# Rotated heads stored the other way round, fewer and larger stack transfers, and a new order of work at the layer borders

## What is computed

```python
xn = layernorm(x)
x = x + attn0(xn, Wq, Wk, Wv, Wo) + ffn0(xn, w_gate, w_up, w_down)      # 16 heads of 32, causal, rotary; hidden 2048
xn = layernorm(x)
x = x + attn1(xn, ...) + ffn1(xn, gate_w, up_w, down_w, scales)         # 16 heads of 32, causal, rotary; hidden 1408
# ffn(xn) = (silu(xn @ gate.T) * (xn @ up.T)) @ down.T
```

## Time and profile before

| | |
|---|---|
| median of 3 runs | 2055.16 us |
| the profiled execution's own time, and its span | 2055.59 us, 2053.8 us |
| PE, DVE, ACT, POOL busy | 91%, 54%, 52%, 34% of the span |
| mean granted clock of TensorE | 0.958 of full speed |
| DMA | 126.2 MB, 22% of 16 engines' time |

### The profile page before, as it was taken

How to read it: one execution, slowest core, us unless ns; L and a number is a source line. 1 busy time by engine, 2 the same in 40 slices (tenths; PEclk the granted TensorE clock), 3 DMA queues, 4 the chain that set the end, 5 groups by cost and what they waited for, 6 DMA issues and landing times.

```text
span 2053.8 us, 25605 instructions
## 1 busy us (share of the span) xinstructions
PE 1866.4 (91%) x8656; PEld 1347.6 (66%) x8656; DVE 1116.6 (54%) x2432; ACT 1060.1 (52%) x2353; POOL 703.4 (34%) x516
## 2 busy tenths in 40 slices
PE   4999999999899899898889999999988998998987
PEld 3777767775675666656467777776757756575654
DVE  6554647373755564736346465573746636455452
ACT  2464646556256473646425646464652555646363
POOL 3225243242341533333213243534314415233320
PEclk9999999999999899999779999999999999999989
DMA  4213113031130313103213131311401403121201
GB/s 159 67 42 98 42 44 90 27 99 41 52 88 22 87 47 73 42 21 109 72 62 78 37 92 42 84 56 29 122 11 52 101 9 98 42 68 37 66 7 41
DMA packets 59874, 126.20 MB, mean 61 GB/s; under 512 B 9440, under 2 KB 10464, under 8 KB 58720
## 3 DMA queue, kind: packets, MB, share of 16 engines
q1 hardware_dynamic: 59744, 124.57, 22.0%
HBM read 69.48 MB, written 4.19 MB: 36 GB/s over the span
## 4 chain that ended last, share of the span: by engine, by line
PE 69%; DVE 11%; ACT 6%; SPq 5%; issue 5%; POOL 3%; DMA 2%; DVEq 0%; ACTq 0%; POOLq 0%
PE D L905 15%; PE G L905 11%; PE U L905 8%; PE OE L999 7%; PE SS L983 6%; PE OE L905 6%; PE SS L905 6%; SPq L564 5%; PE OE L983 3%; PE OE L962 3%; PE SS L962 2%; DVE OE L826 2%; ACT OE L618 2%; ACT pr L634 2%; DMA QS<-pr 1%
## 5 line engine op out<-in xcount | busy, mean ns | idle before, releaser
L874 DVE TENSOR_TENSOR xres<-D,xres 128x512 f32<-128x512 f32 x352 | 243.1, 691 | 214.1 <-PE D L905 209.7
L634 ACT ACTIVATE pr<-SS 128x512 f32<-128x512 f32 (+3 forms) x512 | 232.2, 501 | 143.8 <-PE SS L983 135.5
L709 POOL TENSOR_TENSOR hl<-tt,hh 128x512 fp32r<-128x512 f32 x108 | 139.0, 1287 | 475.7 <-ACT hh L651 475.7
L618 ACT ACTIVATE OE<-OE,mp 128x384 f32<-128x384 f32 (+3 forms) x256 | 203.4, 795 | 104.9 <-DVE mp L826 104.0
L826 DVE CUSTOM_DVE_ANT_0 OE<-OE,mask 128x384 f32<-128x384 f32 (+3 forms) x256 | 220.5, 873 | 50.6 <-PE OE L962 49.7
L618 ACT ACTIVATE SS<-SS,mp 128x128 f32<-128x128 f32 (+3 forms) x256 | 162.2, 634 | 95.7 <-DVE mp L826 94.0
L728 POOL TENSOR_SCALAR_AFFINE_SELECT pr<-pr 128x512 f32<-128x512 f32 x128 | 81.0, 635 | 378.7 <-ACT pr L634 378.7
L826 DVE CUSTOM_DVE_ANT_0 SS<-SS,mask 128x128 f32<-128x128 f32 (+3 forms) x256 | 167.6, 673 | 64.3 <-PE SS L962 63.0
L905 PE MATMUL G<-xh,wgh 128*128 128x512 f32 x432 | 178.0, 412 | 24.0 <-DVE tt L885 22.8
L983 PE MATMUL SS<-QS,KS 98*128 98x512 f32 (+2 forms) x512 | 182.1, 413 | 14.9 <-ACT pr L634 12.3
L905 PE MATMUL D<-wdh,hh 128*128 128x512 f32 x432 | 174.2, 403 | 19.6 <-DVE xres L874 13.7
(11 more groups left out here) (123 smaller groups left out, 3733.6 us busy)
## 6 DMA issues: line engine op xcount, KB each, us to landing
KS<-pr SPq DMA_DIRECT2D x192, 128.0 KB, 2.3
QS<-pr SPq DMA_DIRECT2D x192, 128.0 KB, 2.3
raw<-in_wgate_dram SPq DMA_DIRECT2D x27, 512.0 KB, 3.7
raw<-in_wup_dram SPq DMA_DIRECT2D x27, 512.0 KB, 3.7
raw<-in_wdown_dram SPq DMA_DIRECT2D x27, 512.0 KB, 3.7
raw<-in_wqk_dram SPq DMA_DIRECT2D x16, 512.0 KB, 4.4
val<-in_x_dram SPq DMA_DIRECT2D x4, 1024.0 KB, 6.9
trig<-in_wv_dram SPq DMA_DIRECT2D x4, 1024.0 KB, 5.6
```

The costliest lines, as they stand in the source:

```text
L618: act.activation(s, s, ACT.Exp, bias=mp[:, c, at:at + 1], scale=-1.0, accum_out=se[:, c, at:at + 1]) \
L634: act.activation(weights(i)[:, h, skip:W], SB[(i * HG + h) % 3][:, skip:W], ACT.Exp, scale=-1.0) \
L709: pool.tensor_tensor(hl[:, fc, :], tt[:, (blk * nfc + fc) % 2, :], hh[:, fc, :].bitcast(F32), ALU.subtract) \
L874: dve.tensor_tensor(xres[:, rt, :], d[:, :], xres[:, rt, :], ALU.add).then_inc(sem["v_dfree"], 1)
```

## The change

- **Order of heads.** The split of the Q and K weights writes its columns in the order (dimension, head) (`heads_apart`), so partition k*4+h of a projection holds dimension k of head h. The shuffle is i ^ 4, and the rotation tables are loaded by four transfers with a partition step of 4 instead of one.
- **Order of the projections.** t = 0 to 3 is now K first half, Q first half, K second half, Q second half. After each `rotate`, SyncE issues three transfers that carry all four heads (128 partitions into 32 by 4 heads by 512 columns): 12 a turn of 256 KB instead of 24 of 128. The first natural score waits for the first six (`d_stack`), the 17th for the others (`d_later`).
- **Borders.** The output products of the last turn's second half become items, in front of the norms. `v_weights` comes after the second norm instead of in front of the first scaled tile. The next layer's first projection and first value product (`early`) are taken out of the opening and put in front of the last down products. `keep` is a transfer from DRAM, issued by SyncE. The chain for 1/sqrt keeps its scratch in the PSUM bank `S[1]`. In the opening, `norm` 5, 6 and 7 stand together behind the second projection.
- **Start.** SyncE loads the first four row tiles one by one, the first Q/K weights and the value weights, and only then sets the semaphores and loads the constants. Only the Q/K weights are split in front of the walk; the other three blocks follow after the first norms (`first`).
- **The logarithm's guess** is two ScalarE instructions; VectorE has none in it.
- **Splits on GpSimd** are cut in instructions of 512 columns.
- **Pieces.** `GU_PARTS` stays 2. All 16 digit strings are new, and the late down pieces of the last group stand after three pieces instead of two. Waits are dropped where a stronger one stands in front (`st`, `gated`, `add`).

```diff
+        def heads_apart(kind, t):
+            return t.rearrange("p (g k h) -> p g h k", h=HG, k=DH) if kind == "A" else t
...
-    items.append([("pv", n - 2), ("pv", n - 1), ("heads", 1)])
+    items += [[("pv", n - 2), ("pv", n - 1), ("heads", 1)] + [("x_next",)] * (l == 1 and not final)] + output(1)
...
-    pieces += g0[:GU_PARTS] + late + g0[GU_PARTS:] + g1[:GU_PARTS]
+    pieces += g0[:3] + late + g0[3:] + g1[:3]
     if l == 0:
         rows = [piece + [("row", 1, rt)] for rt, piece in enumerate(d0)]
         rows[-1] += normal(1)
-        pieces += rows + g1[GU_PARTS:] + output(1) + [piece + [("row", 1, TPC + i)] for i, piece in enumerate(d1)]
+        pieces += rows + g1[3:] + early(1) + [piece + [("row", 1, TPC + i)] for i, piece in enumerate(d1)]
         items += norms(1, range(TPC))
+        items[-3].append(("v_weights", 1))
     else:
         d0[-1].append(("store", 0))
         d1[-1].append(("store", 1))
-        pieces += d0 + g1[GU_PARTS:3 * GU_PARTS]
+        pieces += d0 + g1[3:9]
         if not final:
-            items[-1] += [("x_next",), ("v_weights", 0)]
             items += [[("row", 0, rt) for rt in range(TPC)] + normal(0)] + norms(0, range(TPC))
+            items[-3].append(("v_weights", 0))
             pieces[-1].append(("keep", 0))
-        pieces += output(1) + g1[3 * GU_PARTS:] + d1
-    return opening(l), items, pieces
+        pieces += g1[9:] + (early(0) if not final else []) + d1
+    first = opening(l)
+    if (b, l) != (0, 0):
+        first = [x for x in first if [x] not in early(l)]
+    return first, items, pieces
+def early(layer):
+    return [[("proj", 0, True)], [("values", 0, layer)]]
...
-    return [("stats", layer, 0)] + [("v_weights", 1)] * layer + [("xn", layer, 0), ("xn", layer, 1)]
+    return [("stats", layer, 0), ("xn", layer, 0), ("xn", layer, 1)]
...
+    proj = [("proj", t, True) for t in range(2 * NC)]
+    values = [("values", rt, layer) for rt in range(RT)]
...
+    out = [("row", 0, rt) for rt in range(TPC, RT) if layer == 0]
+    out += [("stats", layer, 1), ("xn", layer, TPC), ("xn", layer, TPC + 1), proj[0], values[0], values[1], ("rotate", 0)]
+    out += values[2:4] + later[0] + [proj[1]] + later[1] + later[2] + later[3] + [("keep", 1)] * (layer == 0) + [values[4]]
+    return out + [*values[5:], ("rotate", 1), proj[2], ("rotate", 2), proj[3], ("rotate", 3)]
+START = [("row", 0, rt) for rt in range(TPC)] + normal(0)
+START += [("v_weights", 0)] + [x for piece in norms(0, range(TPC)) for x in piece] + [("first",), ("keep", 0)]
...
-        ("00500010101001100112021102021111111020010020010000100100000100100001000010010000010010001001000000000",
-         "00700010101001100112021102021111111020010020010000100100000100100001000010010000010010001001000000000",
+        ("01200011000100011003020302110202111010101001000000100101000100100000000010010000010010000011000000000",
+         "00400000100020002012020311111111102001010010010000140010001001000000000010010000010010000011000000000",
...
+            for rt in range(TPC):
+                sp.dma_start(val[:, rt, :], x[0, rt * P:(rt + 1) * P, :]).then_inc(d_tile[rt], 16)
+            load(sp, "A", 0, raw[:, 2, :], "raw2")
+            sp.dma_start(wv_raw, wv[0].rearrange("p (c n) -> p c n", c=KC)).then_inc(sem["d_wv"], 16)
...
-                if t % NC < NC - 1:
-                    return
-                qk = t // NC
+                qk, c = t % 2, t // 2
+                cols = slice(c * W, (c + 1) * W)
                 flats = ((flat_h, flat_h, flat_l), (flat_h, flat_l, flat_h))[qk]
                 sp.wait_ge(sem["g_rl"], n("g_rl", 1))
                 if qk:
                     sp.wait_ge(sem["p_v"], n("p_v"))
-                for h in range(HG):
-                    for r, src in enumerate(flats):
-                        at = slice(r * DH, (r + 1) * DH)
-                        sp.dma_start((QS[at, :, h, :] if qk else KS[at, h, :]).bitcast(F32),
-                                     src[qk][h * DH:(h + 1) * DH, :]).then_inc(sem[f"d_stack{h}"], 16)
+                for r, src in enumerate(flats):
+                    at = slice(r * DH, (r + 1) * DH)
+                    sp.dma_start((QS[at, c, :, :] if qk else KS[at, :, cols]).bitcast(F32), src[qk][:, cols]) \
+                        .then_inc(sem["d_later" if c else "d_stack"], 16)
...
+            def keep(n, c):
+                sp.wait_ge(sem["d_out"], n("d_out"))
+                sp.dma_start(xres[:, c * TPC:(c + 1) * TPC, :], rows(x, n, c, n.batches)).then_inc(sem[f"d_keep{c}"], 16)
...
-                act.wait_ge(sem["v_lse"], n("v_lse", 2))
+                act.wait_ge(sem["a_nat"], n("a_nat"))
+                act.activation(y0[:, :], se[:, c, :].bitcast(I32), ACT.Copy, scale=LN2 / 2 ** 23, bias=-(127 - 0.043) * LN2).then_inc(sem["a_log"], 1)
+                act.wait_ge(sem["a_log"], n("a_log", 1))
                 act.activation(ex[:, :], y0[:, :], ACT.Exp, scale=-1.0).then_inc(sem["a_log"], 1)
...
-                y, a = st[:, c, 0, :], st[:, c, 1, :]
+                y, a, v = st[:, c, 0, :], S[1][:, 0:TPC], S[1][:, TPC:2 * TPC]
...
+                dve.wait_ge(sem["a_exp"], n("a_exp"))
+                dve.tensor_scalar(v, var, EPS, None, ALU.add).then_inc(sem["v_chain"], 1)
...
-                if c == 0 and qb == 0:
-                    pe.wait_ge(sem[f"d_stack{h}"], n(f"d_stack{h}"))
-                if t < 4:
+                if t == 0:
+                    pe.wait_ge(sem["d_stack"], n("d_stack"))
                     pe.wait_ge(sem["v_al"], n("v_al"))
                     pe.wait_ge(sem["a_val"], n("a_val"))
+                if t < 4:
+                    held = 1 if n.turns == 0 else 3
+                    pe.wait_ge(sem["v_swap"], n("v_swap", min(0, t - held)))
                 elif c == 0:
                     pe.wait_ge(sem["a_nat"], n("a_nat", -3))
                 elif t == HG * TPC:
+                    pe.wait_ge(sem["d_later"], n("d_later"))
```

More of the change, by code:

```diff
@@ L229, in opening @@
 def opening(layer):
-    out = []
-    proj = [("proj", t) for t in range(2 * NC)]
-    values = [("values", rt) for rt in range(RT)]
+    proj = [("proj", t, True) for t in range(2 * NC)]
+    values = [("values", rt, layer) for rt in range(RT)]
     later = norms(layer, range(TPC, RT))
-    out += [("row", 0, rt) for rt in range(TPC, RT) if layer == 0]
-    out += [("stats", layer, 1), ("xn", layer, TPC), ("xn", layer, TPC + 1), proj[0], values[0], values[1]] + later[0] + [values[2]]
-    out += later[1] + [values[3]]
@@ L238, in opening @@
-    out += later[2] + later[3] + [("keep", 1)] * (layer == 0)
-    out += [values[4], ("rotate", 0), proj[1], values[5], ("rotate", 1), proj[2], values[6], ("rotate", 2), proj[3], values[7],
-            ("rotate", 3)]
-    out = [("open", x[1]) + x if x[0] in ("proj", "values") else x for x in out]
-    for k, x in enumerate(out):
-        if x[0] == "open":
-            behind = max(0, sum(y[0] == "norm" for y in out[:k]) - max(0, x[1] + 1 - TPC)) if x[2] == "values" else 0
-            out[k] = ("values", x[1], layer, behind) if x[2] == "values" else ("proj", x[1], True)
@@ L247, in opening @@
-    return out
-START = [("row", 0, rt) for rt in range(TPC)] + [("stats", 0, 0), ("v_weights", 0), ("xn", 0, 0), ("xn", 0, 1)]
-START += [x for piece in norms(0, range(TPC)) for x in piece] + [("keep", 0)]
+    out = [("row", 0, rt) for rt in range(TPC, RT) if layer == 0]
+    out += [("stats", layer, 1), ("xn", layer, TPC), ("xn", layer, TPC + 1), proj[0], values[0], values[1], ("rotate", 0)]
+    out += values[2:4] + later[0] + [proj[1]] + later[1] + later[2] + later[3] + [("keep", 1)] * (layer == 0) + [values[4]]
@@ L367, in did @@
             self.b, self.layer = step[1:]
+        if step[0] == "keep":
+            self.n[f"d_keep{step[1]}"] += 16
+        if step[0] == "norm":
+            self.normed[step[1]] = self.n["v_dfree"] + 1
+        if step[0] == "x_next":
+            self.batches += 1
+        if step[0] in ("add_wo", "add_down"):
+            rt = step[1] * TPC + step[2]
+            self.written.setdefault(rt, {})[self.b] = self.n["v_dfree"] + 1
         if step[0] == "turn":
@@ L485, in two_layers @@
         d_first = {k: ctx.enter_context(nc.semaphore(f"d_first_{k}")) for k in SPLITS_OPEN[1:]}
+        d_tile = [ctx.enter_context(nc.semaphore(f"d_tile{rt}")) for rt in range(TPC)]
         def load(sp, kind, at, dst, done):
@@ L750, in row @@
             def row(n, layer, rt):
[L751 to L752 removed]
+                if layer == 0 and rt < TPC and n.batches == 0:
+                    dve.wait_ge(d_tile[rt], 16)
+                elif layer == 0:
+                    c = rt // TPC
+                    dve.wait_ge(sem[f"d_x{c}"], n(f"d_x{c}", 16 * c))
                 else:
```

179 lines of the change are left out of this document (94 added, 85 removed).

## The result

The changed kernel takes 2066.47 us (median of 6, 2063.88 to 2068.21) against 2054.39 (median of 6) of the kernel before, measured beside it: ratio 1.0062, interval 1.0044 to 1.0081. The forecast was 2010, with 8 chances in 10 between 1977 and 2042. It is slower by 12 us, where faster by more than 10 had 0.86. The profiled execution spans 2063.3 us.

What follows compares the result with a forecast made beforehand. PE's fixed order of products plus 187.4 us of waits was taken as the bound. Terms -8 -16.3 -5 -14 -9 -9 -10 +8 +6 +12 = -45.3 took 2055.6 to 2010 us; own range 1992 to 2030, 8 in 10 between 1977 and 2042.

Steps and rivals of the forecast that it cites:

- The failed step: Stack transfers before the first score: each 256 KB transfer was to land in 2.7 us, by a straight line in bytes.
- -16.3: PE's waits for stack transfers: 19.3 us go and 3.0 come; bounds -19 and -12.
- The second half's six ... cost nothing: The six stack transfers of the second column half land during the sixteen first scores, so cost nothing.
- The clock terms: Half clock behind stack waits goes, -5 (bounds 0 and -8); 2, 3 and 4 more sit in border and last-turn terms.
- The start: Before the first projection: chain 2 later, stalls -7.9, scaling -4.2, held scalings +2; sum -8, bounds -3 and -11.
- The guess: Logarithm's guess moved to ScalarE: VectorE's wait and PE's gate-bank waits behind it go, -14; bounds -8 and -18.
- Borders: Layer 0 to 1: second scaled-tile wait goes, -9; batch border: waits 13.4 to 7, plus clock, -9.
- Layer 1's last turns: Pieces spread to the 29th and 32nd score: two turns, -3 waits and -2 clock each, -10; bounds 0 and -20.
- Openings and tables: Three transposes together in four openings, +8; early projections' VectorE step waits for rotation tables at three places, +6.
- Uncovered scores: Six turns run six or seven scores without a piece between; PE waits 2 us in each, +12; bounds 0 and 30.
- The rivals: First: saved waits keep the clock up, 1982, chance 0.19; second: the wait turns up again at VectorE, 2038, chance 0.16.
- the third: Thirteen new gaps of about 2 us in turns, openings and early projections lower the clock, 58 us, 2082; chance 0.05.

Runs made afterwards that it cites:

- spread: The changed kernel with each stack's three parts on every third partition of 96 instead of 32 neighbours each; 2027.6 us, ratio 0.9844.
- form 1: The changed kernel's stack transfer, run behind its last store: 256 KB, 128 source partitions to 32, 2 KB rows, four heads of a dimension behind each other; 133 GB/s.
- form 9: Transfer from 128 partitions to 64, one of twelve SBUF-to-SBUF forms run behind the changed kernel's last store; 137 GB/s.
- forms 3 and 8: Transfers behind the changed kernel's last store: 3, 128 KB from every fourth partition to 32, 4 KB rows, 161 GB/s; 8, pairs of heads, 64 to 32, 166.
- forms 1, 6, 9, 10 and 12: Transfers behind the changed kernel's last store, by partitions: 1, 128 to 32; 6, 128 to 128; 9, 128 to 64; 10, 32 to 128; 12, 32 to 32; 133 to 364 GB/s.

## Why the prediction was wrong

- **The failed step**: "128 KB land in 2.3 us and 1024 KB in 5.0, so by a straight line I take 2.7". Landing measured 7.0 and 9.2. Both rows were of other shapes: 32 partitions to 32, and DRAM to 128 partitions. A transfer's time was read as a function of its bytes. With it fell "-16.3" (waits rose by 35.1 instead, with 1.7 to 6.8 us at each of the twelve turn borders inside the layers) and its bounds, since none came from this shape. "The second half's six ... cost nothing" holds for PE's own wait, 0.8 us once, but they are asked for from 178.63 on, while the first six are still landing, and share the engines with them; what that costs wasn't measured.
- **What it was worth**: with the destination spread, one line, the same kernel takes 2027.6 us, 38.9 under 2066.5. With pairs of heads as well it takes 2011.0, 55.5 under, where the miss is 56.5. That this meets the forecast is partly luck: it is another kernel, with 24 transfers of 128 KB that land after 2.4 us, and other terms were off too.
- **The clock terms**: -5 behind the stack waits and -9 in the border and last-turn terms. PE's busy time rose by 2.7 instead. The borders and last turns have more clock (0.84 to 0.95 in the stretch above; 929.5 to 1015 had 0.84, 935.5 to 1024 has 0.90), but the turn borders lost it again: 82 us at half instead of 17. One of the signs of being wrong, a clock below 1 in layer 0's turns, so came true.
- **The start**: -8; the first projection starts 8.1 earlier. The sum was right and two terms weren't: the chain began 3.7 us later and not 2, and the +2 for held scalings in front of the first projection was hardly there (one took 0.89 for 0.56). GpSimd stood still during this chain, because its splits were over or put off, so here the PSUM scratch isn't what freed it. The second chain tests it: beside a split 0.17 us with the scratch in PSUM and 1.44 with it in SBUF. This agrees with the rule that the prediction cites from the Trainium skill, page "SBUF — State Buffer", section "SBUF: two separate sides".
- **The guess**: -14; alone -17.5. Right in size, but about half of it came through the clock. Gate-bank waits are 14.6, over the 10 that was set as its sign.
- **Borders**: -18. PE's waits for scaled tiles at the first border from layer 0 to 1 fell from 6.8 to 3.6, as forecast, and those at the batch border from 13.4 to 9.4, where 7 was expected and 1.6 belong to the early projection.
- **Layer 1's last turns**: -10. The last one gained 0.5 in the table; the other is in the batch border's column and wasn't taken apart.
- **Openings and tables**: +8 and +6. Both right. PE waits 2.25 or 2.26 us for a scaled tile in each of the four openings. The early projection's VectorE step waited for the tables 26.8 us at three places, 9.8 at most, against the 4 set as a sign of error, but only 2.05, 1.62 and 2.08 of it reached PE.
- **Uncovered scores**: +12. PE's waits for ScalarE at the score banks were 24.4 before and 20.7 in the changed kernel. With the transfers quick they are 36.8 (spread), so the term seems right and hidden behind the late transfers; no run changes that alone.
- **The rivals**: the third (slower, by the clock, 2082) had the sign, and part of its mechanism: at 179.90 PE had waited 1.87 us for the gate bank, and behind it the clock went to half. But of the seven gaps of 2 us that it named in openings and early projections only two were followed by half clock, and PE's busy time rose by 2.7 us where it asked for 58. The Trainium skill, page "TensorE: Matmul & The Clock Gate", section "HAM oscillation", speaks of waits in every round with the clock lowered in each. The trace agrees at the turn borders, which have a wait each (clock 0.83 in 174 to 194, 0.86 in 295.2 to 320.2); for the rest of the turn the clock is back. None of the rivals was a slower transfer.

**The mechanism.** Shown: 32 neighbouring destination partitions with four rows to each, from 128, take 133 GB/s (123 in rows of 4 KB), the same rows to every third partition of 96 take 228, and 128 to 128 takes 364. The Trainium skill, "SBUF — State Buffer", section "Door 1: The DMA port swizzle", gives 16 ports with 8 partitions each and about 27 GB/s a port, and "DMA: Bandwidth & Descriptors", section "The descriptor swizzle", says, for a transfer to 128 partitions, which engine serves which of them. Worked out from these pages, as an estimate, and taking the same split for the 128 source partitions, which neither page says of these forms: in form 1 the 16 engines write 4 ports at a time (109 GB/s), in the spread form 10 to 12, in 128 to 128 all 16 (435). The runs agree in order and roughly in size, also for form 9, 64 partitions at 137; but 133 and 137 lie above the 109 that four ports would allow. That engines and ports were so assigned here no trace shows, and forms 3 and 8 (161 and 166) this count doesn't explain.

## What to carry to other kernels

Price a transfer between two SBUF tiles by a row of its own shape, or bound it by the slowest row of any shape; fewer and larger transfers can be slower than many small ones when their writes crowd into neighbouring partitions. Where the order along the contraction is free, try the destination spread: here every third partition took one line. An order of work is laid out for one speed of transfer: with the slow ones the new orders lost 5 us to the old ones (2066.5 to 2061.3, with the old fourth turns shortened), with a third of the bytes gone they won 30 (2023.1 to 2053.2).

## Not expected of the hardware

The same 1.5 MB in six transfers of 256 KB went from SBUF to SBUF at 133 to 364 GB/s, by nothing but the layout of rows on either side (forms 1, 6, 9, 10 and 12). A saturated stretch of such transfers made the 256 KB loads of `wo` from DRAM, issued behind them, land after 14.0 us instead of 2.9; with the spread destination 4.0.
